# Two attention layers and a mixture of experts on one core: first passes loaded from SBUF, part of the prologue behind the first scores

## The reference, cut to what matters

```python
x = x + attn(layernorm(x))        # q, k, v by one 8x24 weight for every head
                                  # softmax(q k^T / sqrt(8) * strict lower triangle) v, then Wr
x = x + ffn(layernorm(x))         # rope on the input of q and k, causal attention, out_proj,
                                  # layer norm, top 2 of 8 experts of 128x128, layer norm
```

## Time and profile before

| | us |
|---|---|
| median of 3 runs | 794.54 |
| lowest and highest | 791.95, 797.81 |
| the profiled execution, its own time | 797.25 |
| its span in the profile | 795.4 |
| ACT busy, PE busy, DVE busy | 653.0, 677.4, 399.0 |

### The profile page before, as it was taken

The page is one execution under the profiler, slowest core; times in us unless marked ns, Lnnn a source line. Parts: engine busy times, 40 slices in busy tenths (PEclk is TensorE's granted clock), DMA queues, the critical chain, the costliest instruction groups (busy, mean ns, idle before and its releaser), DMA issues. The chain is left out here.

```text
span 795.4 us, 15483 instructions
## 1 busy us (share of the span) xinstructions
PE 677.4 (85%) x5568; PEld 259.3 (33%) x5568; DVE 399.0 (50%) x1113; ACT 653.0 (82%) x738; POOL 324.4 (41%) x635
## 2 busy tenths in 40 slices
PE   5689979888899989988899879989997989899644
PEld 3333323333334333333233323333333323233322
DVE  6363453356445552555236643564534673552684
ACT  1599977899899988899799987999996898997441
POOL 3352235223733334234554444343572532434343
PEclk9699998999999997999999989999997999999885
DMA  7856276535666433424354525334553541320010
GB/s 194 272 193 225 71 237 237 140 108 200 209 206 229 146 108 106 127 81 139 117 204 146 170 98 147 99 109 154 171 173 109 162 146 55 84 80 2 0 40 28
DMA packets 76999, 109.84 MB, mean 138 GB/s; under 512 B 13784, under 2 KB 28256, under 8 KB 76896
## 3 DMA queue, kind: packets, MB, share of 16 engines
q1 hardware_dynamic: 72944, 107.32, 42.5%
q10 hardware_dynamic: 3952, 1.30, 0.7%
HBM read 60.91 MB, written 47.68 MB: 137 GB/s over the span
## 5 line engine op out<-in xcount | busy, mean ns | idle before, releaser
L1501 ACT ACTIVATE probs<-scores,shift 128x1024 f32<-128x1024 f32 x576 | 601.2, 1126 | 78.1 <-PE scores L1306 74.4
L1577 POOL TENSOR_SCALAR_AFFINE_SELECT probs<-probs 128x256 f32<-128x256 f32 (+1 forms) x448 | 199.7, 464 | 388.0 <-ACT probs L1501 387.6
L1331 PE MATMUL acc<-probs,v 128*9 128x512 f32 (+3 forms) x3072 | 321.2, 506 | 12.1 <-ACT num L1426 10.3
L1306 PE MATMUL scores<-qs,ks 32*128 32x512 f32 (+3 forms) x1536 | 184.9, 434 | 39.8 <-ACT probs L1501 36.8
L1306 PEld LDWEIGHTS scores<-qs,ks 32*128 32x128 f32 x1536 | 83.1, 189 | 252.3 <-ACT probs L1501 166.4
L1331 PEld LDWEIGHTS acc<-probs,v 128*9 128x9 f32 x3072 | 59.2, 101 | 134.3 <-issue 73.2
L1624 DVE TENSOR_TENSOR prod<-side,G 128x512 f32<-128x512 f32 x44 | 30.4, 691 | 95.4 <-PE side L1272 80.2
L1272 PE MATMUL side<-we,x1T 128*128 128x512 f32 x92 | 53.5, 664 | 3.7 <-DVE shift L1765 2.4
L1426 ACT ACTIVATE num<-acc 128x512 f32<-128x512 f32 x64 | 38.2, 596 | 7.8 <-PE acc L1331 7.7
L1558 POOL TENSOR_TENSOR moe<-psum 128x256 f32<-128x256 f32 x32 | 23.7, 742 | 39.0 <-DVE psum L1624 28.8
L1533 POOL TENSOR_TENSOR rstd<-rstd,expo 128x4 f32<-128x4 f32 x32 | 34.5, 1077 | 2.7
(11 more groups left out here) (189 smaller groups left out, 616.9 us busy)
## 6 DMA issues: line engine op xcount, KB each, us to landing
ks<-k_dram SPq DMA_DIRECT2D x96, 256.0 KB, 4.4
q_dram<-part SPq DMA_DIRECT2D x64, 256.0 KB, 3.2
qs<-q_dram SPq DMA_DIRECT2D x64, 256.0 KB, 3.2
num_dram<-num SPq DMA_DIRECT2D x60, 256.0 KB, 3.4
k_dram<-part SPq DMA_DIRECT2D x30, 256.0 KB, 3.8
xrow<-in_x SPq DMA_DIRECT2D x16, 256.0 KB, 4.3
nat<-num_dram SPq DMA_DIRECT2D x15, 256.0 KB
rdenb<-rden_dram SPq DMA_DIRECT2D x15, 256.0 KB
```

Source lines behind the costliest of these rows:

```text
L1306: ins = pe.matmul(dst, ks[u][r, kt // TH, (kt % TH) * P:(kt % TH + 1) * P], qs[u][r, q0:q0 + w], start=True, stop=not shifted)
L1331: ins = pe.matmul(acc[h * VW:h * VW + VC, q0:q0 + w], v9[V_OF[k]][:, kt, :, HG * hg + h], src, start=(s == 0), stop=last, skip_group_check ...
L1501: act.activation(dst, src, ACT.Exp, bias=shift[:, column(st):column(st) + 1], scale=SCALE).then_inc(probs_raw, 1)
L1577: ins = pool.affine_select(out=blocks, in_=blocks, compare_op=ALU.is_ge, fill=0.0, base=a - 1, pattern=[[0, blocks.shape[1]], [1, P]], cha ...
```

## The change

- **q and k of passes 0 and 1** are copied from `part[0]` to `qs` and `ks`, SBUF to SBUF. SP issues 4 DMAs for q as soon as `q 0` has been read, then 2 for k; ACT issues the 2 others of k ahead of `k_out`. Each moves 128 KB. They stand ahead of `parts_out` of the first half, whose 4 DMAs still go out, since later passes use the copy in DRAM. Pass 2 is loaded right after `parts_out 0`, once all has landed.
- **The prologue's order**: `rows 0` stands ahead of `pairs` on DVE, and `q 0` ahead of `roots`.
- **PE** leaves `k 1`, `v 1`, `suffix 1` and `suffix 0` until the first scores are out: `k 1` and `v 1` behind set 0, `suffix 1` behind set 1, `suffix 0` behind set 3. The part of `k 1` that ACT did is DVE's. Scores wait for each pair of banks by itself (`PAIR_FREE`), and `k 1` is written into bank 4, which belongs to unit 2.
- **`iota8`, `cos`, `sin`** are issued by SP after `parts_out` of the second half, with a semaphore of their own that DVE waits for at `rope0` and at the first choice of experts. ACT's queue ends with `l2b`.
- **The planner** starts DVE and SP at 5.0 and places no job before set 4.
- DVE waits for the straight copies before `part[0]` is written again.

```diff
-BEFORE_TURNS = ([..., ("p1", 0, "root", 1), ("p0", 0, "pairs", 0),
-                 ("p1", 0, "rows", 0), ("p1", 0, "xT", 0), ("p0", 0, "bound", 0), ("p1", 0, "rows", 1), ("p0", 0, "roots", 0),
-                 ("p1", 0, "q", 0), ("p1", 0, "k", 0), ...
+BEFORE_TURNS = ([..., ("p1", 0, "root", 1),
+                 ("p1", 0, "rows", 0), ("p0", 0, "pairs", 0), ("p1", 0, "xT", 0), ("p0", 0, "bound", 0), ("p1", 0, "rows", 1),
+                 ("p1", 0, "q", 0), ("p0", 0, "roots", 0), ("p1", 0, "k", 0), ...
+BEFORE_BANKS = {("p1", 0, "xT", 0): 1, ("p0", 0, "pairs", 0): 0, ("p0", 0, "bound", 0): 2, ("p1", 0, "q", 0): 3, ("p1", 0, "k", 0): 0,
+                ("p1", 0, "xT", 1): 4, ("p1", 0, "q", 1): 5, ("p1", 0, "k", 1): 4}
+BEHIND = {("p1", 0, "k", 1): 0, ("p1", 0, "v", 1): 0, ("p1", 0, "suffix", 1): 1, ("p1", 0, "suffix", 0): 3}
...
-    clock = {"PE": 0.0, "ACT": 0.0, "DVE": 0.0, "POOL": 0.0, "SP": 0.0}
+    clock = {"PE": 0.0, "ACT": 0.0, "DVE": 5.0, "POOL": 0.0, "SP": 5.0}
...
-        room = True
+        room = g > max(BEHIND.values())
...
+        STRAIGHT = 2
+        def q_straight(engine, gp, i):
+            src = part[0][32 * gp:32 * gp + 32, 0, i, :].bitcast(F32)
+            engine.dma_start(qs[gp][i::2, :].bitcast(F32), src.unsqueeze(1).broadcast_to([32, 2, HALF])).then_inc(qs_in[gp], 16)
+        def k_straight(engine, gp, i):
+            engine.dma_start(ks[gp][i::2, 0, :].bitcast(F32), part[0][32 * gp:32 * gp + 32, 1, :, :].bitcast(F32)).then_inc(qs_in[gp], 16)
...
             for x in BEFORE:
+                if x[:4] == ("p1", 0, "parts_out", 0):
+                    sp.wait_ge(side_free, done(("p1", 0, "q", 0)))
+                    for gp in range(STRAIGHT):
+                        for i in range(2):
+                            q_straight(sp, gp, i)
+                    sp.wait_ge(side_free, done(("p1", 0, "k", 0)))
+                    for gp in range(STRAIGHT):
+                        k_straight(sp, gp, 0)
                 if x[5]:
                     turn(*x[:4])
                 if x[:4] == ("p1", 0, "parts_out", 0):
-                    load(0)
-                    load(1)
+                    load(2)
+            sp.dma_start(iota8[:, :], bc(iota8_d)).then_inc(late_weights_in, 16)
+            for t, d in ((cos, cos_d), (sin, sin_d)):
+                sp.dma_start(t[:, :, :], d.rearrange("(t p) f -> p t f", p=P)).then_inc(late_weights_in, 16)
             loads = {}
-            for gp in range(2, NP):
+            for gp in range(3, NP):
...
-                if g == 0:
-                    pe.wait_ge(side_free, N_SCORES)
-                elif last >= PAIRS:
+                for unit in UNITS_OF[g]:
+                    if unit < PAIRS:
+                        pe.wait_ge(side_free, PAIR_FREE[unit])
+                if last >= PAIRS:
...
             for x in BEFORE:
-                turn(*x)
+                if x[:4] not in BEHIND:
+                    turn(*x)
...
+            def behind(g):
+                for x in BEFORE:
+                    if BEHIND.get(x[:4]) == g:
+                        turn(*x)
...
                         scores_set(g, shifted)
+                    if not shifted:
+                        behind(g)
```

31 lines of the change are left out of this document (22 added, 9 removed), and 2 rows, old and new, of the table BEFORE_TURNS.

## The result

The changed kernel took 808.44 us, the median of 4 executions (802.4 to 812.44), against 796.11 for 4 of the kernel before (791.95 to 797.81): a ratio of 1.017, with a 95% interval of 1.0123 to 1.0218. It is slower by 12 to 14 us, where 4 us of gain were forecast; the prediction gave a loss of over 1% a chance of 0.04. The profiled execution took 806.15, with a span of 804.3.

What follows compares the result with a forecast made beforehand. ACT's exponentials were taken as the pace. Terms -6.6 + 1.5 + 3.5 - 2.3 = -3.9 us took the profiled 797.25 to 793.35; less 2.7 for the median, 790.6 us, with 784.0 to 798.5 for 8 in 10.

Steps and rivals of the forecast that it cites:

- Part 4: Later jobs that the planner places elsewhere: taken as 0, with 3 us to either side.
- Part 1: Path to the first scores: they come at 19.5 instead of 26.12, 6.6 us won (4.9 to 8.5).
- Part 2: Work moved behind the first scores: 1.5 us of new ACT gaps (0.5 to 5).
- Part 3: SP's queue, late for x and pass 3's load: 3.5 us of gaps, 1.5 of which stood there before.
- What bounds the kernel: Whole run: ACT's exponentials set the pace; time won ahead of the first counts, less new gaps behind it.
- rival (b): Prologue: straight copies are slow, first scores at 21.2, 1.7 us less won, 792.3 us; chance 0.12.
- the two cases weighed: PE's clock behind the first scores: kept, with gaps of 1.5 us (taken), or 1.2 GHz, with near 5.
- The drain of the tiny runs: SP's ring: tiny runs of cos and sin delay pass 3's load and x by their whole drain.
- (c): SP's queue too late: k 1 read late holds pass 3 and x, transposition at 48.7, 797.0 us; chance 0.12.
- (d): First change of slot: it falls otherwise and its gap of 5.41 us closes, 785.2 us; chance 0.10.
- three warnings: Wrong if first scores pass 22, clock is 0.50 while ACT awaits set 1, or unit 20's gain goes by first slot change.

Runs made afterwards that it cites:

- experiment 1: The changed kernel with the planner starting DVE and SP at 0.0 (the old plan), so later turns keep the order of the kernel before: 799.39 us, 1.0043.
- Experiment 18: As experiment 1, but the writes of q and k to DRAM wait until the straight copies have landed: 800.32 us, 1.0043.
- experiments 4: As experiment 1, with iota8, cos and sin issued by ACT again, at the end of its own broadcasts: 800.49 us, 1.0045.
- experiment 5: As experiment 1, with SP loading batch 1's rows ahead of parts_out 0 and those of p2 0 behind the load of pass 2: 798.08 us, 1.0024.
- experiment 17: As experiment 10, with each block that DVE's branches skip cut to one instruction: 766.07 us, 0.9617.
- experiment 9: The kernel before, with the next batch's x loaded early, its statistics behind suffix 1 and its rows ahead of DVE's branch: 793.85 us, 0.9992.
- Experiments 3: As experiment 1, with k 1, v 1 and the suffix sums ahead of the first scores again: 797.76 us, 1.003.
- 6: As experiment 5, with DVE's first branch over the exact path, and that path's code there, left out: 787.2 us, 0.9894.
- experiment 2: The kernel before with only the planner changed: DVE and SP start at 5.0, no job before set 4 (the new plan): 805.1 us, 1.0077.
- experiment 15: As 12, without DVE's branches over the exact path: 778.96 us, 0.98.
- experiments 14: As experiment 10, with DVE's branches and exact code left out at all ten stretches: 765.04 us, 0.9645.
- 12: As experiment 10, with the planner starting DVE and SP at 5.0 (the new plan): 807.88 us, 1.0173.
- experiment 10: The changed kernel with the old plan, the next batch's x loaded early, its statistics behind v 1 and rows ahead of DVE's branch: 790.11 us, 0.9956.
- experiment 16: As 12, with POOL's squares of p2 1 one set later, so they don't run beside DVE's rows: 802.56 us, 1.012.
- 13: As experiment 10, with DVE's first branch taken inside its wait for k 1 and the turns behind it in both arms: 789.77 us, 0.9938.

## Why the prediction was wrong, step by step

The forecast was 0.995 of the kernel before and the measured ratio is 1.017, a miss of 2.2% or 17.5 us. Two steps failed. About 10 us of the miss are Part 4, the plan taken as 0. The other 7 stand in experiment 1, the change with the old plan (1.0043): they are the landing of k in Part 1 (1.8), the gaps of Part 2 (0.9), and Part 3, whose sum of 3.5 knew SP's queue and not DVE's branch, and where ACT's wait is 8.30 with the old plan.

**What bounds the kernel** held. ACT's progress decides, and its waits for scores more than cover the loss: +12.5 us of wait in a profiled execution that took 8.9 us more.

**Part 1, 6.6 us won: right in its mechanism, 4.85 in size.** The chain ran as laid out, up to the copies: q's were issued at 13.38 (13.3 forecast), SP's of k at 16.02 (16.1). First scores came at 21.27, at the far end of the bounds (21.2), not at 19.5. One term was short, the landing. k's copies took this long from issue (min, median, max; L891 of the profile after), and the one of SP that pass 0 needs, issued at 16.02, about 5.1:

```profile
DMA to landing us min/median/max: 4.2/5.1/5.7
```

I took 3.4, saying that the last copy has the engines nearly to itself. It hasn't: `k_out` is issued at 16.45 and `parts_out` at 17.76, 1.5 MB between them. Experiment 18 takes these away, and its first scores come 0.9 us before the changed kernel's and 1.4 before experiment 1's. What is left, 20.40 against 19.5, fits rival (b). Here are the same experiment's stretches (columns as in the earlier trace rows); the writes are issued from 21.1 on, so that hardly anything but straight copies moved:

```profile
16.00:18.00 2.00, 0.97 (x2) 0.14 (x2) 1.90 (x3) 0.00 (x0) 0.00 (x0) 1.00 0.86 203
18.00:20.00 2.00, 0.00 (x0) 0.00 (x0) 0.55 (x1) 0.00 (x0) 0.00 (x0) 0.72 0.96 193
```

and beside them the changed kernel's, once the writes of 128 partitions move:

```profile
22.00:24.00 2.00, 2.00 (x7) 0.97 (x4) 0.00 (x0) 1.81 (x2) 0.41 (x1) 0.50 1.01 388
24.00:26.00 2.00, 1.52 (x17) 1.33 (x15) 1.85 (x3) 0.40 (x2) 0.41 (x1) 0.88 0.25 96
```

The engines are as busy, at half the rate: 193 against 388 GB/s. The Trainium skill (SBUF — State Buffer, Door 1: the DMA port swizzle) has 32 partitions reach 8 of the 16 ports; the trace agrees with a halving, though of the best rate and not of the 246 from which I had reckoned. No run separates the 32 source partitions from the other thing that is new about these copies, that they go from SBUF to SBUF, so the ports as the cause are argued and not shown.

**Part 2, new gaps of 1.5 us: near, by another route.** The gap ahead of unit 2 was 1.86 us, where 0.8 was forecast, and with the two behind it (0.27 and 0.25, forecast 0.3 and 0.4) the part is 2.4. I took the clock as kept; it was 0.50 from 22 to 24 us (the row above), after 4.41 us in which PE stood idle waiting for k, and `k 1` took 2.08 us instead of 0.98. Of the two cases weighed this was the other, yet its price of 5 was too high: the granted clock was back at 0.88 in the next two microseconds.

**Part 3, SP's queue: the place right, the cause wrong.** x was issued at 36.09 (34.5 forecast) and the transposition ran at 45.39, inside the 45 to 47 forecast. Its gap cost ACT 3.44 us, where 2 was forecast with 4 as the far end; pass 3's load, taken at 1.5, cost nothing: from 26 to 60 us ACT waited 6.3 us for scores, in the gaps named above and one of 0.45. That the sum of the part, 3.5, is met by 3.44 is luck. So is the transposition's hit: experiments 4 and 5 issued x 1.8 and 16 us earlier than experiment 1 and gained nothing. The transposition waits for DVE's statistics, and these wait for DVE to get over the exact path's code: 4 to 6.4 us of "issue" each time, which experiment 17 puts down to the size of the skipped block.

In the kernel before, the same idle stretch lay under the wait for x (7.74 in the earlier trace rows); experiment 9, where x is there in time, has it as 5.31 of "issue". I read that row's releaser as the whole of it. In the changed kernel itself x did come last: it landed at 40.0, where the branch alone would have held DVE to 36.5 to 38.9 (an estimate from the 4.05 to 6.43 us of the experiments, counted from the end of DVE's copy at 32.4). So late x and branch lay over each other, and taking away the first alone wins nothing. The drain of the tiny runs, which the prediction puts ahead of pass 3 and x by ring order, delayed neither: q's load of 34.93 landed 2.7 us after issue, within. The earlier trace rows doesn't test that rule: behind those tiny packets of ACT's queue the writes began to move at 17 in SP's queue as well as in ACT's.

Taking x's path as an SP matter, I charged only SP with a branch (1.8), and DVE with none. The consequence is what cost the early gain: the next batch's first job comes at 42 to 45 us whatever the first scores do, and a start 4.85 us earlier only makes ACT reach that wall sooner. Experiments 3 (start late, same pass 1) and 6 (wall taken away, 4.9 us sooner than 5) show it from both sides, with the old plan.

**Part 4, the plan: 0, with 3 to either side. This is the largest step that failed.** Without it the result would stand at the inner edge of the range: 1.0043 of 794.54 is 798.0, against 798.5. The price of the new order was +6 us under the old prologue (0.77% in experiment 2), 10 under the new one (1.70% less 0.43% in experiment 1), 14 to 18 under the mended ones (experiments 15 against 14, 12 against 10). I had no row for it and gave it the smallest term. The evidence that it could be large stood in the profile all the same: ACT's 74.4 us of waits were spread over 85 places, each of which can change with the order. In the new order one late set of rows at pass 17 makes ACT wait 5.04 us, and that is the DVE and POOL meeting, of which experiment 16 gives back 2.7 net. The other large one is DVE's wait for ACT's tiny operations ahead of `xT` (experiment 15's rows: 4.60 us of ACT), read from the traces alone. What makes up the rest is open.

**The rivals.** (c), SP too late, had the right side and stopped at 797.0: the price was short since it had neither the branch nor the plan in it. (d), the change of slot falling otherwise, had the place of a large cost right and the lever wrong: the gap of 5.41 stands in the changed kernel too (5.96 at 119.44), and it goes with the size of the skipped blocks (experiments 14 and 17), not with the order. Of the three warnings in the prediction's close two came true. The clock was 0.50 while `k 1` held up set 1, and the early gain was gone sooner than the warning said: the lead of 5 us went with pass 2.

**A version that beats both kernels** came out of it: experiment 10 (0.9956 [0.9918, 0.9993]), and 13, not to be told from it (0.9938 [0.9899, 0.9978]). It is the change with the old plan and the next batch's rows ahead of the branch. By the ratios it is worth 3.5 to 5 us against the kernel before, and the interval of 10 only just leaves out no gain. That this is about what was forecast for the change itself is chance, since the added edit does it.

## What to carry to other kernels

A change that reseeds a planner or reorders later work has to be priced as two changes, and the reordering is run alone first: here it cost 6 to 18 us, where the whole change was to win 4. Before counting an earlier start as gain, look for the next fixed point behind it, and read an "idle, released by X" row as the latest of several causes; a branch over much unused code, on an engine that issues in order, is one that no semaphore shows. When several engines' helper work is packed into sets, see which pairs meet, since an operation's time in one place isn't its time beside another.

## What the runs showed of the hardware

- **Skipping a large block costs, skipping one instruction hardly.** DVE stood idle for 4.05, 6.05 and 6.43 us at the first branch over the exact path, and for 4.96 and 4.50 us in the changed kernel at 113 and 209 us; with a block of one instruction the first costs 1.16. The ten blocks cost some 24 us (790.11 against 766.07), more than anything that this change touched. In experiment 5, one packet of q14 moved in each of the microseconds 36, 37 and 38 of the idle stretch, while the data queue held over 90% of the DMA engines up to 38; q14's packets took 3.1, 5.0 and 1.9% of the same 16 engines, so code is fetched over the same engines as data. The Trainium skill (Runtime: NRT & Kernel Launch, Instruction fetch mechanics) says that a taken branch out of the prefetched window must wait for a DMA of its target. The trace agrees, and gives the price. How much of the idle time is the load on the DMA engines wasn't tried.
- **DVE beside POOL.** Four `TENSOR_SCALAR` of 128x128 took 4.10 us beside POOL's two squares and 1.52 without them. The Trainium skill (SBUF — State Buffer, Who interferes with whom) has a `tensor_scalar` of VectorE in a two-port mode and an instruction of GpSimd share a port pair, which the first to issue holds for its whole length while the other is blocked. The trace agrees, with 2.6 us here; in which mode these four ran no run shows.
- **Straight copies.** Copies of 128 KB from 32 partitions, SBUF to SBUF, ran the DMA engines at 0.86 to 0.96 with 193 to 203 GB/s, and writes from 128 partitions to DRAM at 1.01 with 388.
- **Spread.** Ten executions of experiment 1 on one chip reached from 793.64 to 805.13, 1.4%, so that half a per cent needed ten executions and more.
